# State-space steps over two states of 64 channels, and the next batch's transposes in the masked attention's tail

## The reference

```
h[t,d,n] = exp(delta[t,d] * A[d,n]) * h[t-1,d,n] + delta[t,d] * x[t,d] * B[t,n]
y[t,d]   = sum over n of h[t,d,n] * C[t,n]  +  D[d] * x[t,d]
out      = (y * silu(z)) @ W_out
```

## Time and profile before

| | |
|---|---|
| median of three runs | 4474.77 us |
| profiled execution, its own time | 4484.72 us |
| its span, first to last instruction | 4483.1 us |
| PE busy | 3851.2 us, 86% |
| DVE busy | 3082.2 us, 69% |
| ACT busy | 2302.9 us, 51% |
| POOL busy | 2285.0 us, 51% |
| mean granted TensorE clock | 0.934 |
| moved by DMA | 272.99 MB |

### The profile page before, as it was taken

One profiled execution on the slowest core, in us unless ns is written; L12 is line 12 of the kernel. 1 busy time (PEld: TensorE's weight loads), 2 busy tenths in 40 slices (PEclk: granted clock), 3 DMA queues, 4 the chain that ended last, 5 costly groups with the idle time before them and its releaser, 6 DMA issues.

```text
span 4483.1 us, 48003 instructions
## 1 busy us (share of the span) xinstructions
PE 3851.2 (86%) x15760; PEld 2035.4 (45%) x15760; DVE 3082.2 (69%) x4131; ACT 2302.9 (51%) x4201; POOL 2285.0 (51%) x1206
## 2 busy tenths in 40 slices
PE   7979889789779995799999999999999987887786
PEld 3444444444469992233333333333343333444443
DVE  3556547545631112699999999999999998546646
ACT  4455445544622223666667666666666663332433
POOL 2344335433500004588888787778787785220220
PEclk9999999999989996899999999999999999788788
DMA  6000000000078872011111111111111121000000
GB/s 225 20 6 11 20 15 9 12 15 10 28 286 311 318 298 92 22 35 34 49 34 41 35 48 36 38 36 39 43 36 38 36 92 31 1 10 11 9 1 10
DMA packets 102383, 272.99 MB, mean 61 GB/s; under 512 B 9776, under 2 KB 55728, under 8 KB 96400
## 3 DMA queue, kind: packets, MB, share of 16 engines
q1 hardware_dynamic: 97216, 256.75, 17.2%
q0 software_dynamic: 4944, 13.51, 0.9%
HBM read 237.32 MB, written 32.90 MB: 60 GB/s over the span
## 4 chain that ended last, share of the span: by engine, by line
PE 37%; POOL 18%; DVE 18%; issue 15%; ACT 9%; SPq 1%; DMA 0%; POOLq 0%; DVEq 0%; ACTq 0%
POOL AR L672 11%; PE PS L1450 8%; DVE AR L1940 7%; PE PS L1337 6%; DVE PS L1934 4%; PE PS L1393 4%; POOL AR L773 3%; PE PS L1347 3%; PE PS L1364 3%; PE PS L1170 3%; ACT AR L1036 3%; PE PS L1178 2%; PE PS L1197 2%; PE PS L1210 2%; PE PS L1443 1%
## 5 line engine op out<-in xcount | busy, mean ns | idle before, releaser
L773 POOL TENSOR_TENSOR AR<-AR 128x1024 f32<-128x1024 f32 x512 | 1217.5, 2384 | 415.0 <-DVE AR L1940 338.5
L1940 DVE TENSOR_TENSOR_SCAN AR<-AR,PS 128x1024 f32<-128x1024 f32 x512 | 1170.5, 2286 | 17.6
L672 POOL TENSOR_TENSOR AR<-AR,rden 128x1024 f32<-128x1024 f32 x320 | 606.1, 1895 | 974.1 <-DVE rden L1671 907.9
L1450 PE MATMUL PS<-AR,ident 128*128 128x512 f32 x2048 | 1023.9, 627 | 30.8 <-POOL AR L773 30.8
L1036 ACT ACTIVATE AR<-AR,mcol 128x511 f32<-128x511 f32 x1024 | 668.1, 712 | 140.2 <-DVE AR L1940 137.7
L1934 DVE TENSOR_TENSOR PS<-AR,PS 128x1024 f32<-128x1024 f32 x512 | 627.9, 1226 | 79.1 <-PE PS L1435 60.1
L1450 PEld LDWEIGHTS PS<-AR,ident 128*128 128x128 f32 x2048 | 371.1, 194 | 478.0 <-issue 412.6
L1210 PE MATMUL PS<-ident,AR 128*128 128x128 f32 x2560 | 380.3, 296 | 107.8 <-POOL AR L672 91.5
L1210 PEld LDWEIGHTS PS<-ident,AR 128*128 128x128 f32 x2560 | 300.0, 150 | 354.4 <-POOL AR L672 220.6
L1197 PE MATMUL PS<-AR 32*128 32x512 f32 (+1 forms) x1280 | 317.3, 709 | 45.0 <-ACT AR L827 11.5
L837 ACT ACTIVATE AR<-PS 128x512 f32<-128x512 f32 x320 | 189.8, 593 | 302.6 <-PE PS L1210 301.9
(11 more groups left out here) (259 smaller groups left out, 4681.0 us busy)
## 6 DMA issues: line engine op xcount, KB each, us to landing
AR<-in_xw SPq DMA_DIRECT2D x39, 3072.0 KB, 10.5
AR<-mid_cs SPq DMA_DIRECT2D x256, 256.0 KB, 3.3
mid_xs<-AR SPq DMA_DIRECT2D x32, 512.0 KB, 7.9
AR<-mid_xs SPq DMA_DIRECT2D x39, 128.0 KB, 9.6
mid_ys<-AR POOLq DMA_DIRECT2D x39, 128.0 KB, 8.0
AR<-in_ctx SPq DMA_DIRECT2D x8, 512.0 KB, 5.0
AR<-in_mask SPq DMA_DIRECT2D x4, 1024.0 KB, 5.3
mid_x<-AR SPq DMA_DIRECT2D x8, 512.0 KB, 3.0
```

The costliest lines, as they stand in the source:

```text
L672: pool.tensor_tensor(probs[:, i % 4], probs[:, i % 4], rden[:, i % 4, :].rearrange("p (q o) -> p q o", o=1).to_broadcast([P, 2, 512]), ALU ...
L773: pool.tensor_tensor(m_HC[:, W % 3], m_H[:, W % 3, :].rearrange("p (c s) -> p c s", c=2), m_cb[:, n % 4:n % 4 + 1, :].to_broadcast([P, 2, ...
L1450: ins = pe.matmul(PS[:, 2 * hf + c, :], ident[:], m_HC[:, W % 3, c, :], start=False, stop=n == NS - 1)
L1940: v.tensor_tensor_scan(m_H[:, W % 3, :], m_dA[:, W % 4].rearrange("p c s -> p (c s)"), PS[:, 4:6, :].rearrange("p c s -> p (c s)"), 0.0, A ...
```

## The change

**State-space block.** A step now holds two states for one chunk of 128 channels: partitions 0 to 63 carry state 2q, partitions 64 to 127 state 2q + 1, and the free dimension holds the chunk's two halves of 64 channels, again 2 x 512. A chunk takes `NP` = 8 steps, and the chunks follow each other, so there are still 32 steps. Delta and delta x have to lie in both halves of the partitions: SP copies them from one place to another in SBUF with DMAs of 128 KB (`both_states`, four for a chunk of each) into rings of two chunks (`m_dlr`, `m_dur`). C is fetched by two broadcast DMAs of 128 KB a step. B is spread by two products of 64 columns in every step. `add_up` multiplies by `fold`, 128 rows by 64 columns, which adds the two states, once for each half of the output's partitions; all of a step's products go to one bank. `direct` is issued chunk by chunk.

`gated` moves from DVE to POOL, in steps 4 and 6, on copies that ACT (`taken_y`) takes out of PSUM in steps 1 and 2. DVE's step waits first for the scan, then for the fill (every eighth step) and the spread; `residual` moves between product and scan. The turns of bank 7 and the steps of the preparation are others: ACT takes z before the softplus work of the same step, and POOL's `delta` and `delta_x` of the second half move into steps 0 and 2 of the item itself. `conv_weights` and `direct_weights` of the first set are made before the expert loop.

**First layer.** XP takes the place of R. The next batch's x is transposed at the end of the masked attention, its context after the transposes of the attention's output, both moved by ACT, and its first query projection goes ahead of the normalised X's transposes. The zeroing DMAs read b_V.

**Before the experts** ACT moves the first token transposes ahead of the rounding, and PE waits only for the means (`wmean_ok`).

```diff
-O_SLOT = (8, 10, 13, 18)
-Z_SLOT = (20, 21, 23, 24)
+O_SLOT = (10, 11, 12, 15)
+CV_SLOT, CV_OUT = (0, 2, 3, 4, 6, 7, 8, 9), (3, 5, 8, 10)
+D_SLOT = {4: 1, 5: 2, 7: 3}
+Z_SLOT = (21, 23, 24, 25)
+NP = 8
+FILL_DL, FILL_DU = {8: 2, 16: 3}, {3: 1, 11: 2, 19: 3}
...
-            def c_spread(j, n):
-                if 4 * j + n // 4 > 0:
-                    sp.wait_ge(d_hc, 2 * (N_STATE * j + n - 3))
-                sp.dma_start(m_cb[:, n % 4, :], d["cs"][j % 2][n:n + 1, :].to_broadcast([P, 512])).then_inc(ld_c[n % 4], 16)
+            def c_spread(j, w):
+                W = N_STEP * j + w
+                if W >= 4:
+                    sp.wait_ge(d_hc, W - 3)
+                for s in range(2):
+                    n = 2 * (w % NP) + s
+                    sp.dma_start(m_cb[64 * s:64 * s + 64, w % 4, :],
+                                 d["cs"][j % 2][n:n + 1, :].to_broadcast([64, 512])).then_inc(ld_c[w % 4], 16)
+            def both_states(ring, filled, src, c, k):
+                for s in range(2):
+                    for half in range(2):
+                        sp.dma_start(ring[64 * s:64 * s + 64, k, half, :], src[64 * half:64 * half + 64, c, :]).then_inc(filled[k], 16)
+            def fill_delta_x(j, c):
+                G = CI * j + c
+                sp.wait_ge(d_du, 2 * j + c // 2 + 1)
+                if G >= 2:
+                    sp.wait_ge(d_bx, NP * (G - 1))
+                both_states(m_dur, fl_du, m_du, c, G % 2)
...
+                pool.tensor_tensor(fold, ident[:, 0:64], ident[:, 64:128], ALU.add)
...
-                if w in (28, 30):
-                    delta_x(j, w // 2 - 14)
+                if w == 27:
+                    delta_x(j, 0)
...
+            def gated(i, hf):
+                h2 = slice(2 * hf, 2 * hf + 2)
+                if hf == 0:
+                    pool.wait_ge(d_sz, i + 1)
+                pool.wait_ge(d_yc, 2 * i + hf + 1)
+                z = m_sz[i % 2][:, h2, :]
+                pool.tensor_tensor(z, z, y_of(i)[:, h2, :], ALU.mult).then_inc(d_yz, 1)
...
+            def taken_y(i, hf):
+                if i < N_ITEM - 1 and hf == 0:
+                    act.wait_ge(d_lin, 2 * (i + 2))
+                if i == N_ITEM - 1:
+                    act.wait_ge(d_yz, 2 * i)
+                act.wait_ge(d_y, N_STEP * i + 2 * NP * (hf + 1))
+                act.activation(y_of(i)[:, 2 * hf:2 * hf + 2, :], PS[:, 2 * hf:2 * hf + 2, :], ACT.Copy).then_inc(d_yc, 1)
...
+                if q == 0:
+                    act.wait_ge(fl_dl[G % 2], 64 * (G // 2 + 1))
...
+            def next_T(b, u, src):
+                pe.wait_ge(ld_x, b * 32 + 32)
+                for t in range(T):
+                    for c in range(KC):
+                        ins = pe.transpose(PS[:, 4 + c, t * P:(t + 1) * P], src[:, t, c * P:(c + 1) * P], ident[:])
+                ins.then_inc(nx_ps, 1)
...
+                if following is not None:
+                    pe.wait_ge(nx_ev, following * 2 + 1)
+                    next_T(following, 1, ctx_tok)
+                    pe.wait_ge(bo_ev, b * T + T)
+                    first_query(following)
                 tr(b, TR_LNB, X, ln=1)
...
-            pe.wait_ge(dve_set, 2)
+            pe.wait_ge(wmean_ok, 1)
...
+            def spread(W):
+                i, q = W // N_STEP, W % NP
+                if W:
+                    pe.wait_ge(d_bx, W)
+                if W % N_STEP == 0:
+                    pe.wait_ge(d_bc, i + 1)
+                for s in range(2):
+                    ins = pe.matmul(PS[64 * s:64 * s + 64, 6, :], sel[64:128, 2 * q + s:2 * q + s + 1].to_broadcast([64, 64]),
+                                    m_bc[i % 2][64:128, :], start=True, stop=True)
+                ins.then_inc(d_bb, 1)
...
-                for c in range(2):
-                    ins = pe.matmul(PS[:, 2 * hf + c, :], ident[:], m_HC[:, W % 3, c, :], start=False, stop=n == NS - 1)
+                for half in range(2):
+                    ins = pe.matmul(PS[64 * half:64 * half + 64, c, :], fold, m_HC[:, W % 3, half, :],
+                                    start=False, stop=q == NP - 1)
...
             def step(W):
                 i, w = W // N_STEP, W % N_STEP
-                n, hf = w // 2, w % 2
-                if w < 2:
-                    v.wait_ge(d_du, 2 * i + hf + 1)
-                if hf == 0:
-                    v.wait_ge(d_bb, i * NS + n + 1)
+                G, q = W // NP, w % NP
                 if W:
                     v.wait_ge(d_scan, W)
-                v.tensor_tensor(PS[:, 4:6, :], m_du[i % 2][:, 2 * hf:2 * hf + 2, :],
+                if q == 0:
+                    v.wait_ge(fl_du[G % 2], 64 * (G // 2 + 1))
+                v.wait_ge(d_bb, W + 1)
+                v.tensor_tensor(PS[:, 4:6, :], m_dur[:, G % 2],
                                 PS[:, 6:7, :].to_broadcast([P, 2, 512]), ALU.mult).then_inc(d_bx, 1)
+                if i > 0 and w - 1 in O_SLOT:
+                    residual(i, O_SLOT.index(w - 1))
                 v.wait_ge(d_bx, W + 1)
...
-                    if i > 0 and w < 2:
-                        gated(i - 1, w)
```

More of the change, by code:

```diff
@@ L317, in decoder @@
         m_xc = ar([P, CI, 512])
-        m_dl = [ar([P, CI, 512]) for k in range(2)]
-        m_du = [ar([P, CI, 512]) for k in range(2)]
+        m_dl = ar([P, CI, 512])
+        m_dlr = ar([P, 2, 2, 512])
+        m_du = ar([P, CI, 512])
+        m_dur = ar([P, 2, 2, 512])
         assert ar.at == 34316
@@ L577, in _ @@
             c_out(0)
+            fill_delta(0, 0)
+            fill_delta(0, 1)
+            fill_delta_x(0, 0)
             for i in range(N_ITEM):
                 l, b = i // B, i % B
-                for n in range(N_STATE):
-                    c_spread(i, n)
-                    if n == 14 and (i + 1) % B == B - 1 and l + 1 < NL:
+                for w in range(N_STEP):
+                    c_spread(i, w)
+                    if w in FILL_DL:
+                        fill_delta(i, FILL_DL[w])
+                    if w in FILL_DU:
+                        fill_delta_x(i, FILL_DU[w])
+                    if i + 1 < N_ITEM and w == 28:
+                        fill_delta(i + 1, 0)
+                    if i + 1 < N_ITEM and w == 31:
+                        fill_delta(i + 1, 1)
+                        fill_delta_x(i + 1, 0)
+                    n = w // 2 if w % 2 else -1
+                    if w == 28 and (i + 1) % B == B - 1 and l + 1 < NL:
                         sp.wait_ge(sh_ps, turn(i, "z3") + 1)
@@ L783, in _ @@
                     weighted(N_STEP * i + w)
+                    second_half(i, w)
+                    if i > 0 and w in (4, 6):
+                        gated(i - 1, w // 2 - 2)
                     if i + 1 < N_ITEM:
                         start_of(i, w)
+            for hf in range(2):
+                gated(N_ITEM - 1, hf)
             for r in range(B // 2):
@@ L1068, in _ @@
                         opening(i, w)
+            for hf in range(2):
+                taken_y(N_ITEM - 1, hf)
             def ln_e(b, i):
@@ L1461, in _ @@
                     W = N_STEP * i + w
-                    if w % 2 and W + 1 < N_STEP * N_ITEM:
-                        spread((W + 1) // 2)
+                    if W + 1 < N_STEP * N_ITEM:
+                        spread(W + 1)
                     if W >= 2:
+                        if w in D_SLOT:
+                            direct(i, D_SLOT[w])
                         add_up(W - 2)
-                    if 1 <= w < 3:
-                        direct(i, w - 1)
+                    if w == 1:
+                        direct(i, 0)
                     if i + 1 < N_ITEM:
@@ L1963, in _ @@
                     step(N_STEP * i + w)
[L1964 to L1969 removed]
+                    if i + 1 < N_ITEM and w in (19, 22):
+                        capped(i + 1, w // 22)
                     if w == 13 and i + 2 < N_ITEM:
                         inverse(i + 2)
[L1972 to L1973 removed]
             for t in range(T):
```

294 lines of the change are left out of this document (164 added, 130 removed).

## The result

The changed kernel takes 4379.41 us (median of four runs, 4372.04 to 4384.17) against 4476.52 for the kernel before (4473.61 to 4480.6): a ratio of 0.9781, 95% interval 0.9764 to 0.9798, 97 us faster. The forecast was 4359, range 4335 to 4428. Side and size are right; 18.5 us of the gain that was forecast (115.5) are missing. The profiled execution took 4372.04 us, its span is 4370.3, its mean granted clock 0.903.

What follows compares the result with a forecast made beforehand. DVE was taken to set the pace of the state-space stage, with PE close behind. Terms of -87, +1.5, -18, -7 and -5 sum to -115.5 us, giving a median of 4359 us, range 4335 to 4428.

Steps and rivals of the forecast that it cites:

- Part 1: State-space steps on DVE: gating leaves (-56 us), scan wait first (-18), residuals 0, floor 1855 us against 1955.6.
- The scan wait: DVE's state-space steps: scan wait written first makes every step 3.58 us, 256 x 0.07 = -18 us.
- Part 2: PE under the state-space stage: 97 us of PE per item, about 84% busy; stage 1868 us, so -87.
- the 13 us of stalls: State-space stage: DVE's waits for PE's spread, 13 us left (bounds 3 and 60) of today's 29.5.
- Part 3: Work put on POOL, ACT and SP's DMAs in the stage: hidden, except +1.5 us at the last item's end.
- the 6 us of cover: State-space stage: time in hand for the tightest fill, the next item's first product tile.
- Part 4: First layer's batch edges: transposes and query projection fill PE's idle time, three edges, -18 us (bounds -6 and -24).
- Part 5: Two other edges: first expert product earlier, -7 us; z's eviction pulled ahead in front of the stage, -5 us.
- A: Rival: add-up halves don't run side by side, or the spread queue holds DVE; -15 instead of -87, 4432 us; chance 0.11.
- B: Rival: PE idles more in the stage and its clock falls; with four low-clock steps per item 4551 us; chance 0.06.
- C: Rival: late fills behind broadcast DMAs that wait for POOL, 1 us at each of 64 tiles, 4423 us; chance 0.10.
- D: Rival: edges outside the state-space stage give nothing, the stage does; 4389 us; chance 0.06.

Runs made afterwards that it cites:

- e2: Kernel before with the product's scan wait written ahead of its two other waits; 4474.39 us, ratio 0.998 to the kernel before.
- e4: Changed kernel with the add-up again as two products of 128 columns, zeros beside the folding matrix; 4503.38 us, ratio 1.0046 to the kernel before.
- e3: Changed kernel with input weights loaded at step 27 instead of 28 and the last stage's eight loads spread over the last item; 4371.26 us, ratio 0.9751.
- e11: Changed kernel run and profiled again, unedited; 4377.89 us, ratio 0.9777 to the kernel before.
- e12: Changed kernel with bulk loads apart, last item's gating on DVE, two added PE products a step in its steps 18 to 31; 4353.52 us, ratio 0.9722.
- e1: Changed kernel with the product's scan wait written behind its other waits; 4421.67 us, ratio 0.9866 to the kernel before.
- e6: Changed kernel with ACT copying the first token transpose behind the rounding of the weights, as before; 4397.36 us, ratio 0.9807 to the kernel before.
- e7: e3 with four added PE products a step in steps 0 to 9 and 18 to 31 of the last item; 4414.78 us, ratio 0.9845.

## Why the prediction was right, and what it missed

**Part 1, DVE's steps.** The gating term (-56) holds: steps 0 and 1 give 3.7 us x 16 = 59. (6.1 us was the mean of step 0 over 16 items; over the 15 edges it is 6.29.) The scan wait (-18) was mis-sized: every step is 3.58 as said, but 256 steps of 3.65 was wrong, there were 115 of them, so -8 at most (e2). Residuals between product and scan: 0 holds, 3.77 to 3.82 before and 3.78 to 3.81 after, the last item left out. But I had read 0.15 us for one, and it is 0.2, and a capping is 0.46 and not 0.42. Fifteen plain items of 116.4 us and a last one of 115.3 make the floor 1861 us and not 1855.

**Part 2, PE.** Right in kind and nearly in size. At the full clock a group of four records lasts 1.08 us and the next product begins 1.0 after its start (1.06 forecast); the spread takes 0.33 (0.41), so its halves run side by side as well. The 0.311 us of the group holds the records at the low clock. The change of form costs what was read: behind an add-up the first 128*128 record is 0.53 us ahead of the second, else 0.43, both fp32. Over a plain item PE is busy 102.7 of 116.4 us, 88%, and not 97 us and 84%. e4 shows that this form carried the change: without it the kernel is 0.5% slower than the one before. The term that failed is the 13 us of stalls: they are 24. Of these 11.3 are the input weights at step 29 (with item 6's step 30), 9.8 the last item's, and only 3 are what I had in mind, PE late by its own work. This is 11 of the 16 us that the stage lacks; the floor is 5 or 6 more.

**Part 3.** POOL's 1626.7 us busy and ACT's 1296.7 cost nothing in plain items, as said, and no fill was ever late: the 6 us of cover held, at a DMA share of 0.40. What I left out is SP's other work. A broadcast of C is now issued when POOL comes to the step three before its own, where it was three states, six steps; so all that stands behind it in SP's order is issued later. The input weights and the product that reads them, item 2 of the kernel before:

```profile
2171.03 0.38 SPq L534 DMA_DIRECT2D AR<-in_m_win  x1
```
```profile
2184.72 1.88 PE L1364 MATMUL PS<-AR 128*128 128x512 f32 x4
```

The load had 13.7 us before PE came; after, it is issued at 2133.24 and PE stands before it from 2135.1 on, 1.9 us later, while it takes 5.6 to land (5.0 before). Measured against the scans the load leaves 10.0 us later. SP in the trace after shows that the broadcasts are the smaller part of it:

```profile
2116.86 10.37 SPq L576 DMA_DIRECT2D AR<-mid_cs  x6
2130.79 2.40 SPq L582 DMA_DIRECT2D AR<-AR  x4
2133.24 0.59 SPq L546 DMA_DIRECT2D AR<-in_m_win  x1
```

The broadcasts of step 28 are out at 2127.23, 4 us later than the load before. The other 6 us are the fill L582, which the change put ahead of the load at step 28: it waits until POOL has made the next item's delta (L792, ended at 2130.77), and its four issues take 2.4 us. At step 27 (e3) the load stands ahead of that fill and leaves 6.9 us earlier. The diff showed both waits, and I followed them for fills and broadcasts alone. In the last item it is the same on a larger scale: at step 3 SP waits for POOL's delta (L792, ended at 3565.25) and issues the eight loads until 3571.4, and the broadcast of step 4 behind them is due when POOL ends step 3 at 3574.5. It lands behind 5.2 MB, which are 13.5 us at the 386 GB/s of that window. The tail is +4.0 us and not +1.5: at the low clock the last add-up takes 1.97 and not 1.08 us (+0.9) and the first out-projection 3.75 and not 1.96 (+1.8). These rows are from the trace after, in order of time, behind the last scan's end at 3681.11:

```profile
3683.58 1.97 PE L1584 MATMUL PS<-AR,upper 128*64 128x512 f32 x4 [2.50 <-POOL AR L833]
3685.66 1.02 ACT L1128 ACTIVATE AR<-PS 128x1024 f32<-128x1024 f32 x1 [16.61 <-PE PS L1584]
3686.77 2.34 POOL L842 TENSOR_TENSOR AR<-AR 128x1024 f32<-128x1024 f32 x1 [0.94 <-ACT AR L1128]
3689.21 3.75 PE L1558 MATMUL PS<-AR 128*128 128x256 f32 x8 [3.65 <-issue]
```

**Part 4, the edges.** From the first gate product to the fourth 908.9 us before and 888.4 after, -20.5 over three edges (-18 forecast); the projections start 3.1 us behind the gate product, where it was 9.8.

**Part 5.** First expert product: 42.6 to 34.7 us behind the gate product, -7.8, of which -5.4 is left at the second tile (-7 forecast): ACT's rounding now runs between the first tile's product and its Silu. The prologue (-5) gave nothing: between the first convolution product and z's first product it takes 47.3 us (46.3 before), and from there to the stage 37.9 in both. The pulled z cut PE's wait from 6.2 to 4.7 us, and ACT loads its tables ten times between the convolution and the stage instead of six. The -11.3 of the marks lies in front of the first convolution product and is nothing that the forecast named; whether it is chance or the changed kernel's own stays open (e11).

**The baseline.** I took the change against a profiled execution and subtracted it from the median. The sum came out well against the profiles, -115.5 for -112.8, but partly by luck: 21 us of that lie in two stretches where nothing that the forecast named gained, and of which one (9.7) varies by itself. The profiled execution before was 8 us above its median and the one after 7 below. Stage (-70.9), edges and experts (-24.9) and tail (+4.0) make -92, with the stretch in front of the stage (-11.3) -103; the medians' -97 lies between. The low end of the range, 4335, was a slip as well: its bounds give 4338.

**The rivals.** A didn't happen; forced, it costs more than I gave it (e4). B happened where I had not looked: items 0 to 14 lost tenths of a us to it at most, but the stage's clock fell to 0.89, under the 0.9 that I had named as a sign, and the last item, without companion work, lost 4.8 us at steps 10 and 15 and 2.7 in the tail. PE's low clock in the trace goes with PE idling: 20.68 of 28 us busy at 0.50, and 1.00 with added work (e12). The Trainium skill ("TensorE: Matmul & The Clock Gate", Part 1) says that the gate follows how busy PE is; these two windows agree. C's mechanism, DMAs that land late, is what took the rest, with bulk loads in the place of fills, one of them behind a fill: 16 us (e3) and not the 64 of its price. D is out: edges and experts gave what was forecast.

## What to carry to other kernels

When a change doubles the DMAs of a stage or shortens its step, follow how far ahead the queue that issues them now runs, and look at every other load in it and at what now stands ahead of that: here SP ran three steps ahead instead of six, a new fill that waited for POOL stood in front of a 1 MB load, the bulk loads cost 16 us, and moving one of them by a single step, to the other side of the fill, took its part away. Write the wait that comes last in steady state first, and count in the trace in how many steps it really is the last one. Where an engine's companion work ends (the last item here), its clock can fall and the tail runs at half speed; a little work that nobody needs, sized to fit under the bounding engine, bought 5 us of the tail in the one profile taken, and sized wrongly cost 42.

## What the runs showed of the hardware

- **A wait costs by its place.** On DVE a wait written behind the first adds 0.07 us to a step when it is the scan's own: 3.58 against 3.65 over 512 steps, 38 us. The Trainium skill ("Perfetto Trace Analysis", Identifying Dependency Chains) says that instructions that wait for several engines may have EventSemaphore instructions with the further waits put ahead of them; the traces agree (the records at 2406.48 and 2408.46 under e1), and the steps give the price.
- **Two products of 64 columns side by side.** Two fp32 products of 128x64 by 128x512 into the two halves of the partitions start 6 ns apart, and the next product begins 1.01 us after them (trace after, 2406.36 to 2407.37). Two of the whole width at the same place, behind the spread, take 1.82 us (e4, 2402.20 to 2404.02). Both at the full clock.
- **ACT stands still towards the end of POOL's gathering.** In front of the stage ACT stood still for 9.9 to 10.6 us in seven of the fourteen traces and for 6.1 and 6.4 in two, although its operand was there. It had worked beside the same gathering DMAs until then. In the trace of e1 and in that after, the same instructions:

```profile
1711.93 0.60 ACT L1025 ACTIVATE AR<-PS 128x512 f32<-128x512 f32 x1 [9.91 <-issue]
```
```profile
1705.21 0.60 ACT L1025 ACTIVATE AR<-PS 128x512 f32<-128x512 f32 x1 [2.07 <-PE PS L1497]
```

  PE had ended its product at 1704.06 in e1. In the traces of e1, e6 and e7 ACT went on 1.6 to 1.8 us after POOL's last gathering DMA had ended, in that of the kernel before (idle 10.6 us, are behind it) 2.5 us after; but in e4 (6.1 us) it went on 2.6 us before that end, and in the two traces of the changed kernel it did not stop. What holds it stays open; it accounts for 8 of the 14 us by which this stretch varies.
